# Plain attention phase: heads in pairs, periods of one key tile, one reduction for two heads' maxima, the next batch projected in the last quad

## What is computed

```python
q = (src @ Wq + bq).reshape(B, T, 16, 16)      # src = xn, 16 heads of 16
k = (src @ Wk + bk).reshape(B, T, 16, 16)
v = (src @ Wv + bv).reshape(B, T, 16, 16)
probs = softmax(einsum('bqhd,bkhd->bhqk', q, k) * 16 ** -0.5)
attn = einsum('bhqk,bkhd->bqhd', probs, v).reshape(B, T, 256) @ Wo + bo
x1 = layer_norm(src + attn, ln1_g, ln1_b)
```

## Time and profile before

| | |
|---|---|
| median of three runs | 2310.1 us |
| profiled execution: device time | 2310.43 us |
| its span, first to last instruction | 2308.6 us |
| mean granted TensorE clock | 0.939 |
| busy: PE, PE weight loads, DVE | 1958.1, 1220.4, 1359.2 us |
| busy: ACT, POOL | 958.1, 953.9 us |
| plain phase | 0 to 809 us: start 50, seven periods of a batch 670, last batch and end 89 |

### The profile page before, as it was taken

How to read it: one execution, slowest core, us unless ns; L and a number is a source line. 1 busy time by engine, 2 the same in 40 slices (tenths; PEclk the granted TensorE clock), 3 DMA queues, 4 the chain that set the end, 5 groups by cost and what they waited for, 6 DMA issues and landing times. The chain is left out here.

```text
span 2308.6 us, 37690 instructions
## 1 busy us (share of the span) xinstructions
PE 1958.1 (85%) x12145; PEld 1220.4 (53%) x12146; DVE 1359.2 (59%) x2919; ACT 958.1 (42%) x1361; POOL 953.9 (41%) x761
## 2 busy tenths in 40 slices
PE   6888988889888706999759998999989999898997
PEld 3454554545545305888635454655546455454654
DVE  4665766657666443667576565655546655465561
ACT  3655656556565412344214334142332424324142
POOL 4322130221302153344345637456373754638454
PEclk9999999999999857999969999999999999999999
DMA  6400000000000053555330010100101000010000
GB/s 205 156 9 0 9 9 0 9 0 9 9 0 1 0 211 123 198 206 183 115 85 1 1 38 1 38 1 1 38 1 38 1 10 29 1 38 1 17 12 10
DMA packets 56173, 104.81 MB, mean 45 GB/s; under 512 B 7238, under 2 KB 46566, under 8 KB 50156
## 3 DMA queue, kind: packets, MB, share of 16 engines
q1 hardware_dynamic: 52972, 94.71, 12.1%
q0 software_dynamic: 3072, 8.39, 1.1%
HBM read 76.35 MB, written 26.74 MB: 45 GB/s over the span
## 5 line engine op out<-in xcount | busy, mean ns | idle before, releaser
L368 POOL TENSOR_TENSOR a_probs<-a_probs 128x512 f32<-128x512 f32 x288 | 360.4, 1284 | 348.1 <-PE a_psO L686 347.1
L517 DVE CUSTOM_DVE_ANT_0 a_junk<-a_psM,a_alibi 128x512 bf16<-128x512 f32 x512 | 333.8, 689 | 236.1 <-PE a_psM L646 213.9
L1157 DVE TENSOR_REDUCE f_q_tok<-f_psR 128x1 f32<-128x512 f32 x512 | 336.4, 688 | 151.7 <-PE f_psR L1276 150.8
L451 ACT ACTIVATE a_probs<-a_psS 128x1024 f32<-128x1024 f32 x256 | 249.2, 1022 | 360.0 <-PE a_psS L672 270.5
L1118 ACT ACTIVATE f_probs<-f_psS 128x1024 f32<-128x1024 f32 x256 | 262.5, 1033 | 107.6 <-PE f_psS L1296 107.2
L1276 PE MATMUL f_psR<-f_kZ,f_qM 128*128 128x512 f32 x512 | 236.4, 491 | 39.4 <-DVE f_q_tok L1157 15.8
L686 PE MATMUL a_psO<-a_probs,a_v 128*32 128x512 f32 x2048 | 260.3, 631 | 0.0
L1000 POOL TENSOR_TENSOR f_oT<-f_oT,f_rsum 128x512 f32<-128x512 f32 x32 | 41.0, 1281 | 350.2 <-DVE f_rsum L1168 350.2
L1276 PEld LDWEIGHTS f_psR<-f_kZ,f_qM 128*128 128x128 f32 x512 | 101.1, 198 | 158.3 <-DVE f_q_tok L1157 94.7
L1296 PE MATMUL f_psS<-f_qS,f_kZ 128*128 128x512 f32 x512 | 177.2, 431 | 5.9 <-ACT f_probs L1118 5.2
L646 PE MATMUL a_psM<-a_kH,a_qH 64*128 64x512 f32 x512 | 129.7, 503 | 42.8 <-DVE a_n_tok L517 42.4
(11 more groups left out here) (199 smaller groups left out, 3880.8 us busy)
## 6 DMA issues: line engine op xcount, KB each, us to landing
w_w_high<-w_parts SPq DMA_DIRECT2D x19, 1024.0 KB, 5.4
w_w_low<-w_parts SPq DMA_DIRECT2D x19, 1024.0 KB, 7.4
sorted_x<-f_zeros SPq DMA_DIRECT2D x1, 4864.0 KB, 19.9
e_xs<-sorted_x SPq DMA_DIRECT2D x19, 256.0 KB, 2.7
sorted_z<-e_z SPq DMA_DIRECT2D x19, 256.0 KB, 2.2
f_xn<-in_L_attn_x SPq DMA_DIRECT2D x8, 512.0 KB, 3.5
f_w_raw<-in_L_ffn_W SPq DMA_DIRECT2D x4, 1024.0 KB, 9.2
w_parts<-f_w_high SPq DMA_DIRECT2D x4, 1024.0 KB, 3.9
```

The costliest lines, as they stand in the source:

```text
L368: nc.gpsimd.tensor_tensor(slot, slot, probs[:, GRP * (j - 1) + e, :], ALU.add).then_inc(added.sem, 1)
L451: nc.scalar.activation(probs[:, slots, :], psS[:, 2 * p:2 * p + 2, :], ACT.Exp).then_inc(exp_done.sem, 1)
L517: nc.vector.tensor_tensor_reduce(out=junk[:, a, :], in0=psM[:, a, :], in1=alibi[:, h, :], scale=1.0, scalar=-3.0e38, op0=ALU.add, op1=ALU.max,
L1157: nc.vector.tensor_reduce(q_tok[:, c, h, NEG:NEG + 1], psR[:, bank_of("max", m), :], AX.X, ALU.max, negate=True).then_inc(max_done.sem, 1)
```

## The change

All of it lies in `plain_attention_phase`.

1. Pairs. `kZ` with its zero rows gives way to `kP`, a tile of 128 rows for a pair, copied by one ACT instruction. A product for one head uses 64 rows of PE, and the two heads of a pair lie on the two halves.
2. Maxima. The ring `psR` gives way to `psM` (two banks, one pair) and `psT` (one bank for transposes). One DVE reduction takes both heads (1024 elements), 32 for each batch instead of 64. The next product for maxima waits until the last reduction is done: there is one `psM`.
3. Periods. A quad is four periods of one key tile. In each: one product pair for maxima ("early"), the scores of two pairs, up to two sets of transposes, a second pair for maxima ("late"), then `weigh` of the period before. Of two sets of transposes one goes to `psT`, the other to a bank of `psS` and so waits for the period's first exponential. `probs` holds two periods.
4. Order over batches. The maxima of a quad start two ahead, so 10 of a batch's 32 are in `prepare` and 22 in the first 11 periods. The next batch's rows and six projections move from `prepare` into the last quad, in banks of `psM`. The values' biases wait for the last `weigh` of the batch, since `v` is one tile. In `prepare`, four sets of four output products lie between the maxima 1 to 5, and none after them.
5. The second norm: statistics on DVE after the first period of the next batch, application on POOL (`finish_rows`). The first norm of the next batch: statistics in period (1, 2), application in (2, 3). POOL splits two parts of `W1` in batch 0 and two in batch 7; SP's loop over batches stands between them.

```diff
-        ring = [(kind, p) for kind in ("keys", "queries") for p in (0, 1)]
...
+    PREPARE = [("keys", 0), ("queries", 0), ("keys", 1), ("queries", 1), ("max", 0), ("keys", 2), ("max", 1),
+               ("queries", 2), ("out", 4), ("max", 2), ("out", 4), ("keys", 3), ("max", 3), ("queries", 3), ("out", 4),
+               ("max", 4), ("shifted", 0), ("out", 4), ("max", 5), ("max", 6), ("max", 7), ("max", 8),
+               ("shifted", 1), ("max", 9)]
...
+        items = [[], [("shifted", 2 * quad + 2), ("keys", 2 * quad + 4)],
+                 [("queries", 2 * quad + 4), ("keys", 2 * quad + 5)],
+                 [("shifted", 2 * quad + 3), ("queries", 2 * quad + 5)]][j]
+        return [(kind, n) for kind, n in items if n < PAIRS]
...
+        first = MQ * (quad + 1) + 2 * j + AHEAD
...
             def take_max(b, m):
-                h, c = divmod(m, TT)
+                pair, c = divmod(m, TT)
                 dve.wait_ge(max_ps.sem, max_ps.at(b, m))
-                nc.vector.tensor_reduce(q_tok[:, c, h, NEG:NEG + 1], psR[:, bank_of("max", m), :], AX.X, ALU.max,
+                nc.vector.tensor_reduce(q_tok[:, c, 2 * pair:2 * pair + 2, NEG], psM[:, :, :], AX.X, ALU.max,
                                         negate=True).then_inc(max_done.sem, 1)
...
+            def multiply_for_max(b, m):
+                pair, c = divmod(m, TT)
...
+                    pe.wait_ge(max_done.sem, max_done.at(b, m - 1))
...
+                for a, half in enumerate(HALVES):
+                    last = nc.tensor.matmul(psM[:, a, :], qM[half, pair % 4, c * P:(c + 1) * P], kP[half, pair, :],
+                                            start=True, stop=True, tile_position=(FB * a, 0))
+                last.then_inc(max_ps.sem, 1)
...
+                for r in range(PERIODS):
+                    quad, j = divmod(r, TT)
+                    rows = more and quad == QUADS - 1
+                    exponentials(b, r, 0)
+                    if rows and j > 1:
+                        high_parts(b + 1, 2 * j - 3)
+                    exponentials(b, r, 1)
+                    for kind, n in side(quad, j):
+                        take[kind](b, n)
+                    if rows and j == 0:
+                        take_xnT(b + 1)
+                    if rows and j in (1, 2):
+                        high_parts(b + 1, 2 * j - 2)
...
+                    if (quad, j) == (0, 0) and before is not None:
+                        dve.wait_ge(r1_done.sem, r1_done.at(before, 1))
+                        norm1.statistics(dve, before, r1)
...
+                    if early is not None:
+                        multiply_for_max(b, early)
+                    for p in range(QP):
+                        scores(b, r, p, taken[p])
+                    taken = [dict(items[:-1]), {}]
+                    if items:
+                        turn_free(b, *items[-1])
+                        transpose_pair(b, *items[-1])
+                    for kind, n in items[:-1]:
+                        pe.wait_ge(exp_done.sem, exp_done.at(b, QP * r))
+                        transpose_pair(b, kind, n)
+                    if late is not None:
+                        multiply_for_max(b, late)
+                    if rows and j == 0:
+                        transpose_rows(b + 1)
+                    if r:
+                        weigh(b, *divmod(r - 1, TT))
+                    if rows and j:
+                        for n in (2 * j - 2, 2 * j - 1):
+                            project(b + 1, n)
```

More of the change, by code:

```diff
@@ L1048, in batch, with quads @@
                 nc.gpsimd.tensor_tensor(x1_b, x1_b, offset, ALU.add).then_inc(x1_done.sem, 1)
-            passes(pool, batch)
+            norm0.raise_variance(pool, 0)
+            reset_maxima(0)
+            pool.wait_ge(loads, LOADS)
+            for t in range(TT):
+                low_parts(0, t)
+            def quads(b, more, before=None, splits=()):
+                xnb_sum(b)
+                if before is not None:
+                    finish_rows(before)
+                for e in splits[0:1]:
+                    split_w1(e)
+                normalize(b, 0)
+                if more:
+                    norm0.raise_variance(pool, b + 1)
+                for e in splits[1:]:
+                    split_w1(e)
+                normalize(b, 1)
+                if more:
+                    reset_maxima(b + 1)
+                normalize(b, 2)
+                if more:
+                    for t in range(TT):
+                        low_parts(b + 1, t)
+                normalize(b, 3)
+            quads(0, True, splits=range(EARLY))
+            with pool.Fori(0, B - 2) as b:
+                quads(b + 1, True, b)
+            quads(B - 1, False, B - 2, splits=range(EARLY, NE))
+            finish_rows(B - 1)
         @block.scalar
@@ L1129, in batch @@
                     prepare(b + 1)
+            take_xnT(0)
+            for t in range(TT):
+                high_parts(0, t)
             prepare(0)
@@ new lines, in scores @@
+            def scores(b, r, p, taken):
+                quad, j = divmod(r, TT)
+                pair = QP * quad + p
+                needs = dict(taken)
+                if j == 0:
+                    needs["shifted"] = max(pair, needs.get("shifted", 0))
+                if r > 0:
+                    pe.wait_ge(exp_done.sem, exp_done.at(b, QP * (r - 1) + p))
+                for kind, n in needs.items():
+                    pe.wait_ge(reader[kind].sem, reader[kind].at(b, n))
+                for a, half in enumerate(HALVES):
+                    last = nc.tensor.matmul(psS[:, 2 * p + a, :], kP[half, pair, j * P:(j + 1) * P],
+                                            qS[half, pair % 4, :], start=True, stop=True, tile_position=(FB * a, 0))
@@ new lines, in batch @@
+            def batch(b, more):
+                taken = [{"shifted": 1, "keys": 3}, {"queries": 3}]
+                for r in range(PERIODS):
+                    quad, j = divmod(r, TT)
+                    items = side(quad, j)
+                    early, late = maxima(quad, j)
+                    rows = more and quad == QUADS - 1
+                    if early is not None:
[8 more added lines that the diff above has]
+                        pe.wait_ge(exp_done.sem, exp_done.at(b, QP * r))
+                        transpose_pair(b, kind, n)
+                    if late is not None:
[5 more added lines that the diff above has]
+                    if rows and j:
+                        for n in (2 * j - 2, 2 * j - 1):
+                            project(b + 1, n)
+                weigh(b, QUADS - 1, TT - 1)
@@ L1376, in batch @@
                         project_output(b, n, False)
+            transpose_rows(0)
+            for n in range(NB):
+                project(0, n)
             prepare(0)
```

402 lines of the change are left out of this document (183 added, 219 removed).

## The result

The changed kernel takes 2327.46 us (median of 4, 2324.42 to 2329.36), the kernel before 2309.99 beside it: ratio 1.0074, 95% interval 1.0056 to 1.0092. It is slower by 17.5 us, where 8.6 less were forecast; the miss is 26 us. The profiled execution took 2329.36 us, its span 2327.3.

A forecast was written before the change was run, and what follows sets the result against it. The PE-DVE hand-over of `psM` replaces PE as bound in the quads. Seven batches -8.7 us, start +5.5, batch 0 -0.8, last batch -5.6, end +0.6: together -9.0, 2301.5 us; range 2278 to 2335.

The forecast's parts named there:

- The term for the clock: PE's clock halves as each preparation ends, costing 0.9 us in three hand-overs and 1.4 in two periods: 2.3 us a batch.
- Pairs, hand-over, periods: Quads: reduction 1.22 us, hand-over cycle 1.82, periods 3.64 or 4.25 us, other DVE work 3.2; eleven periods 46.9 us.
- Rival C: The hand-over costs 0.83 us instead of 0.58, 45 us in all: 2347 us; chance 0.12.
- rival D: The two halves of PE don't run together, 0.2 us a pair, 36 in all: 2337 us; chance 0.02.
- Last stretch: Period (2, 3) and the last quad, where PE is the bound again: laid out at 21.4 us.
- Preparation: From the transposes through the output products and hand-overs to the first period: 24.0 us.
- rival B: The clock falls again within the quads, two or three more periods a batch at 1.2 GHz: 2323 to 2335 us; chance 0.2.
- Rival A: The clock doesn't fall at the preparation's end, or its fall costs nothing: 2283 us; chance 0.2.
- Seven batches: A batch takes 94.6 us against 95.84 before, 1.2 less, so 8.7 us less over seven batches.
- The start: First period begins at 55.2 us instead of 49.78, after ten cycles of 1.82 and 1.2 for the clock: +5.5 us.
- The last batch: Without projections: last stretch 11.8 us, quads 46.1 + 1.4, in all 59.3 us against 64.9, so -5.6.
- The end: The phase's end has the second norm's application on POOL: -0.7 to +1.4 us, taken as +0.6.

The follow-up runs named there:

- e13: Changed kernel plus products nobody reads, only in PE's gaps in the preparation and ahead of second maxima pairs in quad 2: 2297.7 us, ratio 0.9956.
- e9: Kernel before with one POOL wait, for DVE's application of the second norm, moved ahead of the sum of rows: 2292.2 us, ratio 0.9932.
- e15: Changed kernel with unread products in gaps only, second maxima pair ahead of second transposes, last batch's second norm on DVE: 2287.5 us, ratio 0.9910.
- e1: Changed kernel plus unread products in each preparation: two after maxima 6, 7 and 8, one per output step of batch 0: 2314.3 us, ratio 1.0016.
- e10: Changed kernel with 16 unread two-column products ahead of batch 0's first transposes, shifting PE's later code in memory: 2329.0 us, ratio 1.0086.

## Why the prediction was wrong

**What failed, in short.** The term for the clock, 2.3 us a batch for one fall, left out a second fall as the last quad begins; the layout was 1.3 us a batch too short; and the sum set the new kernel against a kernel before whose own loss it never priced.

**Pairs, hand-over, periods.** Right. 1.22, 0.60 and 1.82 us, 3.65 and 4.26 to 4.35 a period, DVE's other work mostly in the slack. That 1.22 came out is in part luck: it was worked out from a reduction of 512 and another DVE instruction of 2048 elements, as POOL's price was from other instructions, and that one came out wrong. In the batch without falls the eleven periods are 46.5 us (46.9 forecast). Rival C, 0.83 instead of 0.58, and rival D did not happen.

**Last stretch.** 22.0 without a fall, 21.4 forecast: 0.6 too little. **Preparation.** 25.1 against 24.0: four intervals with output products at 2.79 instead of 2.45. The durations were taken from single groups, without what lies between a group's first and the next group's first product. Less the 0.4 that the eleven periods were laid out too long, 1.3 us a batch, 9 in all.

**The clock.** Mis-sized: 2.3 us a batch allowed, 3.4 measured (e13), 8 us in all. The text counted one fall, at the preparation's end, with 1.4 us in the first two periods. It left out the fall as the last quad begins, which costs 1.2 to 2.6 us in six batches of seven: from the last maximum to the next preparation's first reduction 27.80 to 29.21 us, where the one batch without it has 26.65 (laid out: 1.29 to the end of the period, 21.4 and 3.45, 26.1). The fall that was counted costs about what was allowed: some 0.8 us in the preparation and 1.0 in the first quad, by the means of the changed kernel against that batch of e13. The one left out costs 1.4 on the mean, and once in the seven batches a third one, among the output products, 1.7. This is rival B's mechanism, the clock falling again within the quads, and B's 2323 to 2335 us hold the result, by luck: B priced two or three full periods at 1.2 GHz and no error in the layout. It does not fall in (0, 2) or later in the full quads, against which the text had spoken with the evidence of the earlier trace rows. It falls behind quad 2's periods without transposes, and there the text never looked. Two of the signs of being wrong that it named came: a last stretch over 22 us (23.37), for the clock and not for the bias chain, and a preparation over 25 (25.99), for the layout first (25.13 without a fall). Rival A's world is e13, 2297.7 us instead of 2283: its price was right in kind, the layout beneath it too short, and falls are left in e13 too. By the Trainium skill's rule ("TensorE: Matmul & The Clock Gate", A second HAM failure mode: psum-queue depth-cycling) 2329 was named; the trace agrees with its kind, a clock that goes up and down between PE's groups, and 2327.5 us are near that number by the same luck.

**Seven batches** thus missed by 18: 9 for the layout, 8 for the clock, 1 because the batch of before was taken as 95.84 where the mean is 95.68.

**The start** was 0.8 off: the ten cycles were at 1.2 GHz nearly throughout (2.12 us), 2.7 us in sum, where 1.2 were allowed. **The last batch** came as forecast. **The end** missed by 2.9: an application on POOL is 1.225 us, taken as 0.24 to 0.735 from two other kinds of instruction in the earlier trace rows. A bound from another instruction's rows was no bound; with four of them on the last chain it should have been wider.

**Nothing behind the phase** was the forecast; 5.7 us came from PE standing there. No row of before could show it.

**What the sum never asked.** It priced the new kernel from below and set it against a batch of before that held a loss of 2.9 us. The text named that loss (POOL's `xnb` in DVE's way, PE's clock 0.97 in the earlier trace rows), but priced neither it nor a kernel that cures it alone. With it cured the old layout needs 93.0 us a batch, and the new one, laid out at 92.3 without the clock, needs 93.6 at full clock and 96.9 as it is. So of the change the norm's move gained 18 us (ratio 0.9924), and pairs, periods and order, with all that hangs on them, cost 35 (from 0.9924 to 1.0074).

## What to carry over

Work taken off a busy PE is no gain where a chain of hand-overs takes its place: PE then waits, its clock falls, and the shorter work comes back at half speed; lay such a schedule out at both clocks, and look at the stretches with the least work in them. Before a large rebuild look for a long instruction beside one on POOL: one wait moved (e9) took 16 us off the kernel before, where the rebuilt kernel with all that helped (e15) is 21 below it. Compare phases by their own ends when the code around them moves, and batches by their own lengths when the start moves too.

## What was not expected of the hardware

- POOL's subtract and multiply with two values per partition, 128x256: 1.225 us. Its additions of the same shape take 0.735, DVE 0.41 for the same.
- Two reductions of 512 back to back take 1.29 us on DVE, one of 1024 takes 1.22.
- Products that nobody reads can put a fall of the clock off (e1), and take most of the falls away (e13: 40 us at 1.2 GHz instead of 172), for 24 us of an 822 us phase.
- In the changed kernel PE stands for 3.1 to 4.4 us, waiting for nothing that the profile shows, once in six of the eight rotary batches; with 16 small products far ahead it doesn't (e10).
